# The scan step of a two-layer selective state-space network: from a ScalarE clamp with B corrections to one saturating add on VectorE

## What is computed

```python
xr, gate = jnp.split(x @ W_in.T, 2, axis=-1)
xc = silu(causal_conv4(xr + t_emb) + b_conv)
xn = layernorm(xc) * ln_g + ln_b                      # 512 channels
Bm, Cm, dt = jnp.split(xn @ W_xproj.T, 3, axis=-1)    # 16 states each
Ad = 1.0 + tanh(dt @ W_dt.T + b_dt) * 0.01 * -tanh(A_log)
Bd = Bm * jnp.minimum(norm(xn), 1.0)
def step(h, inputs):
    ad, bd, xt, ct = inputs
    h = jnp.clip(h * ad[:, :, None] + bd[:, :, None] * xt[:, None, :], -10.0, 10.0)
    return h, jnp.einsum('bd,bdh->bh', ct, h)         # h: 16 states x 512 channels
y = scan(step) + D * xn
x = x + y * silu(gate) @ W_out.T
```

## Time and profile before

| what | value |
|---|---|
| median of 3 runs | 1794.24 us |
| lowest and highest run | 1790.63 and 1795.34 us |
| span of the profiled execution, first to last instruction | 1790.3 us |
| median less the span | 3.9 us |
| TensorE busy | 1677.0 us, 94% |
| VectorE busy | 1623.9 us, 91% |
| ScalarE busy | 1307.1 us, 73% |
| GpSimd busy | 686.9 us, 38% |
| mean granted TensorE clock | 0.988 |

### The profile page before, as it was taken

How to read it: one execution, slowest core, us unless ns; L and a number is a source line. 1 busy time by engine, 2 the same in 40 slices (tenths; PEclk the granted TensorE clock), 3 DMA queues, 4 the chain that set the end, 5 groups by cost and what they waited for, 6 DMA issues and landing times. The chain is left out here.

```text
span 1790.3 us, 43798 instructions
## 1 busy us (share of the span) xinstructions
PE 1677.0 (94%) x14852; PEld 748.9 (42%) x14852; DVE 1623.9 (91%) x2492; ACT 1307.1 (73%) x2213; POOL 686.9 (38%) x702
## 2 busy tenths in 40 slices
PE   6999999999999999889999999999998899999998
PEld 3555555555554555332222224545553322222244
DVE  5899999999987999989999998679999899999975
ACT  5655556455546999889999993069998899999910
POOL 0223233232332332456666650012335576765500
PEclk9999999999999999899999999999998999999999
DMA  4000001000002344554545666624345445455678
GB/s 162 1 2 0 1 2 31 2 1 0 1 1 83 129 161 163 181 172 133 183 150 188 226 188 205 237 84 173 136 175 185 155 137 184 150 189 196 189 235 276
DMA packets 126456, 226.85 MB, mean 127 GB/s; under 512 B 35620, under 2 KB 61220, under 8 KB 117540
## 3 DMA queue, kind: packets, MB, share of 16 engines
q1 hardware_dynamic: 125912, 223.51, 37.9%
q10 hardware_dynamic: 432, 1.84, 0.3%
HBM read 141.95 MB, written 83.36 MB: 126 GB/s over the span
## 5 line engine op out<-in xcount | busy, mean ns | idle before, releaser
L1063 ACT ACTIVATE R<-q,Ast 128x512 f32<-128x512 f32 x1016 | 632.9, 708 | 34.5 <-DVE q L2085 32.3
L2085 DVE SCALAR_TENSOR_TENSOR q<-R,PS 128x512 f32<-128x512 f32 x1008 | 610.3, 677 | 9.6 <-ACT R L1063 5.9
L628 POOL TENSOR_TENSOR Uw<-Ub,rowmask 96x512 bf16<-96x512 bf16 x256 | 335.6, 1345 | 144.0 <-PE PS L1510 131.7
L1510 PE MATMUL PS<-xq,Uw 97*128 97x512 bf16 x1024 | 327.1, 391 | 46.5 <-DVE q L2085 37.8
L1527 PE MATMUL PS<-q,Wy 128*32 128x512 f32 x2016 | 279.8, 610 | 0.4 <-DVE q L2085 0.4
L1510 PEld LDWEIGHTS PS<-xq,Uw 97*128 97x128 bf16 x1024 | 84.9, 97 | 363.5 <-DVE q L2085 271.4
L1178 PE MATMUL PS<-X,Win 128*128 (+1 forms) x456 | 213.6, 606 | 0.1
L1079 PE MATMUL PS<-xn,Wl 128*128 128x512 f32 x384 | 186.6, 609 | 0.8 <-DVE xn L1649 0.7
L549 POOL TENSOR_TENSOR ex<-ex,rs 128x1024 f32<-128x1024 f32 x32 | 76.8, 2401 | 164.2 <-DVE rs L1672 164.2
L1767 DVE SCALAR_TENSOR_TENSOR acc<-xp,Wc,acc 128x512 f32<-128x512 f32 x192 | 134.5, 749 | 2.6 <-DVE eC L1889 0.2
L542 POOL TENSOR_TENSOR vsc<-vTd,vs_t 128x1024 f32<-128x1024 f32 x16 | 41.6, 2601 | 216.4 <-ACT vTd L773 216.4
(11 more groups left out here) (183 smaller groups left out, 2640.9 us busy)
## 6 DMA issues: line engine op xcount, KB each, us to landing
xq<-xpart_d SPq DMA_DIRECT2D x384, 192.0 KB
sg_d<-sg SPq DMA_DIRECT2D x16, 1024.0 KB, 5.3
xn_d<-z SPq DMA_DIRECT2D x16, 1024.0 KB, 3.9
y_d<-ys SPq DMA_DIRECT2D x64, 256.0 KB, 4.0
xnp<-xn_d SPq DMA_DIRECT2D x16, 1024.0 KB, 8.3
sgp<-sg_d SPq DMA_DIRECT2D x16, 1024.0 KB, 11.1
xpart_d<-xh SPq DMA_DIRECT2D x16, 512.0 KB, 2.9
xpart_d<-xmi SPq DMA_DIRECT2D x16, 512.0 KB, 3.7
```

What stands on the lines that cost most here:

```text
L628: pl.tensor_tensor(Uw[0:XROWS, h, w, :, :, :], Ub[0:XROWS, w, 0:N, ds(s0, CH)].rearrange("p n t -> p t n").unsqueeze(2).broadcast_to([XROW ...
L1063: act.activation((end if end and (h, t) == (1, CH - 1) else R)[:, w, :], q[:, t % 2, w, :], ACT.Relu, scale=Ast[:, h, w, t:t + 1], bias=CL ...
L1510: pe.matmul(PS[:, w, :], Uw[0:KROWS, h, w, t, :, :].rearrange("p b n -> p (b n)"), xq[0:KROWS, hb, w, s8 % XT, :], start=True, stop=True). ...
L2085: v.scalar_tensor_tensor(out=q[:, s8 % 2, w, :], in0=R[:, w, :], scalar=2 * CLIP, in1=PS[:, w, :], op0=ALU.min, op1=ALU.subtract).then_inc ...
```

## The change

The state is kept as it is. VectorE does the whole step in one instruction, a custom operation of two tensors and two constants: q = max(min(R + PSUM, 10), -10). ScalarE only scales: R = decay * q, and does so for token n out of the q of token n - 1, right before step n. With it go: the division of B by the decay (GpSimd's four instructions a group, a reciprocal and the factor mr on VectorE), `carried`, `fold_b` on TensorE, the strip `By` and its matmuls and staging, the 97th row, the clamps after the last token. `y_of` reads q of its own token. The x buffers are free as soon as the input matmul has read them, and SP's loads wait for that instead of for `y_of`. The custom instruction stands in no loop: VectorE's eights of tokens are all written out; ScalarE's, TensorE's and GpSimd's loops stay. The copy of y comes one token earlier (after tokens 1 and 5 of an eight instead of 2 and 6).

```diff
-                def over_decay(it):
-                    pl.wait_ge(am_r, it + 1)
...
                 def stage(...):
-                    pl.tensor_tensor(By[0:XROWS, h, :, :, MID:MID + GB],
-                                     Ub[0:XROWS, :, N:NB, ds(s0, CH)].rearrange("p g o t -> p t g o").broadcast_to([XROWS, CH, QW, GB]),
...
-                stage(1, 0, 0)
-                for p in range(2):
-                    pl.wait_ge(ac_r, l * (PASSES * QW * S) + QW * S - QW + 2 * p + 2 + READY)
-                    alone(pl)
-                    pl.tensor_scalar(R_end[:, 2 * p:2 * p + 2, :], R_end[:, 2 * p:2 * p + 2, :], 2 * CLIP, -CLIP, ALU.min, ALU.add).then_inc(ep_q, 1)
-                stage(1, 0, 1)
+                stage(1, 0, 0, True)
+                stage(1, 0, 1, True)
...
-                def clamp(pi, c2, first, between=None, end=None):
+                def decayed(pi, c2, first, between=None):
                     for h in range(2):
                         cn = pi * CHUNKS + c2 * 2 + h
                         act.wait_ge(pl_a, cn + 1)
...
                         for t in range(CH):
                             if between:
                                 between(c2 * 8 + h * CH + t)
+                            if first and h == 0 and t == 0:
+                                continue
                             for w in range(QW):
-                                act.wait_ge(dv_q, cn * (QW * CH) + QW * t + w + 1 + QW)
-                                act.activation((end if end and (h, t) == (1, CH - 1) else R)[:, w, :], q[:, t % 2, w, :], ACT.Relu,
-                                               scale=Ast[:, h, w, t:t + 1], bias=CLIP).then_inc(ac_r, 1)
+                                act.wait_ge(dv_q, cn * (QW * CH) + QW * t + w + 1)
+                                act.activation(R[:, w, :], q[:, (t + 1) % 2, w, :], ACT.Copy,
+                                               scale=Ast[:, h, w, t:t + 1]).then_inc(ac_r, 1)
...
-                def fold_b(it):
-                    pe.wait_ge(rB_r, it + 1)
-                    pe.matmul(PS[:, 7, 0:P], ident[:, :], rB[:, :], start=True, stop=False)
-                    pe.wait_ge(eC_r, it + 1)
-                    pe.matmul(PS[:, 7, 0:P], fold[:, :], eC[:, :], start=False, stop=True).then_inc(tok_mm, 1)
...
                     for p in range(2):
...
                         for w in (2 * p, 2 * p + 1):
-                            mm = pe.matmul(PS[32 * w:32 * w + 32, 4 + h, :], By[0:XROWS, h, t, w, MID - t * GB:MID + (CH - t) * GB],
-                                           xq[0:XROWS, hb, w, xt, :], start=False, stop=(t == CH - 1), skip_group_check=True)
+                            mm = pe.matmul(PS[32 * w:32 * w + 32, 4 + h, :], Wy[:, h, w, t * 32:(t + 1) * 32],
+                                           q[:, s8 % 2, w, :], start=(t == 0), stop=(t == CH - 1), skip_group_check=True)
...
-                    v.tensor_tensor(rB[:, :], PS[:, 6, 0:P], mr[:, :], ALU.mult).then_inc(rB_r, 1)
-                def carried(it):
+                    v.tensor_tensor(rB[:, :], PS[:, 6, 0:P], mn[:, :], ALU.mult).then_inc(rB_r, 1)
...
-                    v.tensor_copy(tvp[:, 0, :], PS[:, 7, 0:P]).then_inc(tv_s, 1)
+                    v.tensor_copy(tvp[:, 0, :], rB[:, :]).then_inc(tv_s, 1)
...
-                        v.scalar_tensor_tensor(out=q[:, s8 % 2, w, :], in0=R[:, w, :], scalar=2 * CLIP, in1=PS[:, w, :],
-                                               op0=ALU.min, op1=ALU.subtract).then_inc(dv_q, 1)
+                        v._custom_dve(bass.dve_ops.TENSOR_ADD_SAT, out=q[:, s8 % 2, w, :], in0=R[:, w, :], in1=PS[:, w, :],
+                                      s0=CLIP, s1=-CLIP).then_inc(dv_q, 1)
...
-                        if s8 == 2 and before:
+                        if s8 == 1 and before:
                             keep_y(pi, c2 * 2 - 1, 1)
-                        if s8 == 6:
+                        if s8 == 5:
                             keep_y(pi, c2 * 2, 0)
...
-                    with v.Fori(plain, CHUNKS // 2) as c2:
+                    for c2 in range(plain, CHUNKS // 2):
                         eight(pi, c2, False, True)
-                pi = l * PASSES + PASSES - 1
-                for p in range(2):
-                    v.wait_ge(ac_r, pi * (QW * S) + QW * S - QW + 2 * p + 2 + READY)
-                    v.tensor_scalar(R[:, 2 * p:2 * p + 2, :], R[:, 2 * p:2 * p + 2, :], 2 * CLIP, -CLIP, ALU.min, ALU.add).then_inc(ep_q, 1)
                 keep_y(l * PASSES + PASSES - 1, CHUNKS - 1, 1)
```

More of the change, by code:

```diff
@@ L155, in cond_resid_kernel @@
         zq = sb("zq", [P, DC, TOK], where=front)
-        rc0 = sb("rc0", [P, P], where=front)
+        sb("rc0", [P, P], where=front)
         zve = sb("zve", [P, P], where=front)
@@ L167, in cond_resid_kernel @@
         mn = sb("mn", [P, P], where=front)
-        mr = sb("mr", [P, P], where=front)
+        sb("mr", [P, P], where=front)
         dts = sb("dts", [P, P], where=front)
@@ L196, in cond_resid_kernel @@
         ys = sb("ys", [P, 2, DI], where=scan)
-        R_end = sb("R_end", [P, QW, DI], where=scan)
+        spare_y = sb("spare_y", [P, QW, DI], where=scan)
         scan.close()
@@ L658, in _ @@
                     alone(pl)
-                    stage(0, 0, h, True)
+                    stage(0, 0, h, True, True)
                 last_parts(l * G + G - 2)
@@ L1055, in clamp @@
                         act.wait_ge(pl_a, cn + 1)
-                        if first and h == 0 and between:
-                            act.wait_ge(pe_yq, pi * (2 * S) + USED)
                         for t in range(CH):
@@ L1069, in _ @@
                     for c2 in range(plain):
-                        clamp(pi, c2, c2 == 0, last_group if ps == 0 else None)
-                    with act.Fori(plain, CHUNKS // 2 - 1) as c2:
-                        clamp(pi, c2, False)
-                    clamp(pi, CHUNKS // 2 - 1, False, end=R_end if ps == 0 else None)
+                        decayed(pi, c2, c2 == 0, last_group if ps == 0 else None)
+                    with act.Fori(plain, CHUNKS // 2) as c2:
+                        decayed(pi, c2, False)
         @block.tensor
@@ L1539, in _ @@
                     for c2 in range(plain):
-                        for s8 in range(1, 9):
+                        for s8 in range(8):
                             if ps == 0:
@@ L1543, in _ @@
                             inputs(pi, c2, s8 + 1, ps == 0 and c2 == 0)
-                            if ps and s8 == 1:
-                                y_of(pi - 1, CHUNKS // 2 - 1, 8, last=R_end, spare=(0, 0))
                             y_of(pi, c2, s8)
                     with pe.Fori(plain, CHUNKS // 2 - 1) as c2:
-                        for s8 in range(1, 9):
+                        for s8 in range(8):
                             inputs(pi, c2, s8 + 1)
                             y_of(pi, c2, s8)
-                    for s8 in range(1, 8):
+                    for s8 in range(8):
                         if s8 < 7:
```

162 lines of the change are left out of this document (58 added, 104 removed).

## The result

| | before | after |
|---|---|---|
| median of 15 runs, us | 1792.12 (1788.21 to 1797.58) | 1798.59 (1794.32 to 1804.05) |
| span of the profiled execution, us | 1790.3 | 1802.3 (its time 1804.05) |
| granted clock of TensorE, mean | 0.988 | 0.981 |

The ratio after to before is 1.0032, with a 95% interval of 1.0021 to 1.0044: slower by 6.5 us, just past what can be told from no change. The forecast was 1779.3 us. So some 19 us are to be explained. None of them lies where I had put most of the risk, in the pace of the custom instruction. A costlier start of pass 0 with less gained behind it was among my rivals, at 0.05 and with 1787 us; the rest I hadn't seen.

What follows compares the result with a forecast made beforehand. The scan was taken to run at VectorE's pace, ScalarE second. Terms 0 - 3.9 + 4.2 - 7.7 - 4.0 - 3.5 = -14.9 us gave a span of 1775.4, median 1779.3 us; range 1769 to 1800.

Steps and rivals of the forecast that it cites:

- A costlier start of pass 0 with less gained behind it: Rival: start costs +8.4 instead of +4.2 us, nothing gained from the reorder at step 17; 1787 us, chance 0.05.
- Steady state: Scan: VectorE's instruction count per token unchanged, custom step at the old pitch of 0.598 us; 0 us.
- The two rivals to which I gave 0.30: Scan: custom instruction clearly slower (0.17; half-way 1809, at most 1839 us) or slightly slower (0.13; 11 ns each, 1790 us).
- Front: Seven bodies a layer: without mr and eC `rows` starts 0.28 us earlier in each; -3.9 us in all.
- The rest of the body hangs on `rows`: Front body: z waits for the spreading of `rows`, so its 0.28 us earlier start counts in full.
- Start of pass 0: ScalarE's `high` and `middle` stand ahead of the R for steps 1 and 2; +2.1 us a layer, +4.2 in all.
- Steps 14 to 17: Pass 0: reciprocal, eC and mr gone from VectorE, `split_b` needn't wait for TensorE's fold; -3.8 us a layer, -7.7 in all.
- ScalarE carries them on: Pass 0 up to step 13: ScalarE, the tighter engine, passes on the start's 2.1 us a layer.
- Between the passes: VectorE's idle time while TensorE's y waits for GpSimd's clamp of the last R goes; -2.0 us a layer, -4.0 in all.
- end: End of the scan: y is copied without waiting for R, the clamp and a second round; -1.75 us a layer, -3.5 in all.
- The written-out loop: VectorE's scan: written-out steps take 9.65 us for sixteen, looped 9.64, so neither branch nor fetch shows; costed at nothing.
- The clock rival: TensorE's clock falls in the scan; 35 tokens at the low level would bring +35 us, 1814, all +256; chance 0.05.

Runs made afterwards that it cites:

- second pair of profiles: Kernel before and changed kernel, each run again with no edit: 1792.1 us, ratio 1.0011, and 1796.4 us, ratio 1.0026.
- run 3: Changed kernel with GpSimd's xlo waiting for VectorE's mean rows instead of rB: 1790.9 us, ratio 0.9988 to the kernel before.
- run 4: Changed kernel with the last group's pieces on ScalarE one token later, behind the decays: 1789.6 us, ratio 0.9972 to the kernel before.
- both edits: Changed kernel with xlo waiting for the mean rows and ScalarE's pieces one token later: 1784.4 us, 0.9957; with VectorE's scan looped, 1780.8 and 1779.9 us.

## Why the prediction was wrong

The measured 1798.6 us lies within the stated range of 1769 to 1800, but by luck: its slow end was made for a slower custom instruction, and that isn't what happened. By the prediction's own steps, with the measured value of the second pair of profiles:

- **Steady state, 0: right.** The pitch is 0.598 us and the loop's turns don't show in the scan. The two rivals to which I gave 0.30, a slower custom instruction, fall with it. So does the sentence from the Trainium skill's "Vector Engine (DVE) Microarchitecture Reference", section 3.4, by which I had estimated 608 ns: sixteen take 9.64 us, and the measurement decides. The sentence there speaks of one kind of custom program, with integer inputs, so it was a distant source.
- **Front, -3.9: wrong, +5.0.** Two things failed. "The rest of the body hangs on `rows`" was wrong: before the change `rows` was done 0.3 us ahead of the projections behind which TensorE spreads it, and run 3 shows what the term is worth without anything else, 0.06 us a body. And I had not asked what GpSimd would do with an earlier release. Run 3, which takes it away, gains 2.5 us a front. Removing eC took away not just its 0.29 us but also the thing that kept xlo off `rows`.
- **The last body and `split_b`.** The source of the casts moved from PSUM to SBUF. I costed that at nothing. In the last body of the front it costs 0.7 us (3.20 instead of 2.54 from the first cast to step 0, beside GpSimd's `Uw`), and in the scan of layer 0 the first cast takes 0.73 instead of 0.29 us, again until GpSimd's `Uw` is through. This is read from the rows; it wasn't tried apart.
- **Start of pass 0, +2.1 a layer: right.** `rows` stands 10.8 us behind step 0 instead of 8.4. Run 4 takes away this very delay.
- **Steps 14 to 17, -3.8 a layer: right in size, wrong in what is left of it.** From am to the start of `split_b` it takes 9.4 us, and took 13.2: -3.8. But am itself stands 47.8 us behind step 0 instead of 44.0. Of these 3.8 us the start explains 2.4; "ScalarE carries them on" was too kind, as steps 4 to 13 add 1.4. And from the start of `split_b` to the last `xr`, VectorE takes 20.6 us instead of 18.5: the casts cost 0.5 more, and the waits for R before steps 17 and 20 are 0.80 and 0.50. "I count all of it" was the error: the same misplaced pieces on ScalarE hold up the later steps too, and run 4, which moves them all, gives 3.8 and 3.9 us in the two layers.
- **Between the passes -2.0 and end -1.75 a layer: right**, 3.9 together.
- **Behind the scan, 0: wrong, +4.0 and -0.6.** No term stood for it. What is shown: it isn't the DRAM place of `ones`, nor the removed loads, nor the custom instruction, nor the written-out loop alone. The full DMA engines move some 30 GB/s less for 30 us, and one instruction packet delays two landings. Why they move less stays open.
- **The written-out loop, 0: too good.** In three pairs with the new program the looped kernel is faster: 5.3 and 3.9 us on one chip each, and 0.9940 against 0.9957 on two; in the old program by 0.9 us, with an interval that takes in 0 and 4. The intervals of the last three pairs overlap, but the sign is the same four times. The scan's own stages don't show it, and I can't say which instructions wait.

In sum the front is 8.9 us off, pass 0 8.1 and the stages behind the scans 3.4, in part through the loop; pass 1 and the start take 0.1 off. From -14.9 that leads to the measured +5.3. The clock rival was not it where I had put it: in the steady scan the granted clock is 1.00. But in pass 0, where steps wait, TensorE is part of the time at the low level, and longer after the change: the mean granted clock there is 0.94 in both layers, against 0.95 and 0.96 before (second profiles), an estimate of 22 and 22 us at the low level against 18 and 14. In run 3, whose pass 0 is 1.1 us shorter with the same code, it is 0.96 and 0.95. So a part of the 1.4 us between steps 4 and 13 may be the clock's; no run separates it from ScalarE's order.

The best version here is the changed kernel with both edits and VectorE's loop kept: 1780 us, 0.9933 of the kernel before, though its interval overlaps those of the written-out versions. That is where the forecast had the change itself, though by other terms.

## What to carry to other kernels

When a change removes an instruction on which another engine waited, ask what that engine starts now, and beside which instruction: the removed wait may have been the spacing between them. Before you count an earlier result as a gain, look at what its consumer has queued ahead of it. And when the engine that feeds the scan gets its work in another order, place each small piece behind the work that the bottleneck waits for; here that was worth 6.7 us, nearly as much as the small instructions and the wait that the change took from steps 14 to 17 (3.8 us in each layer).

## What the runs showed of the hardware

- **Some VectorE instructions with all their tensors in SBUF wait beside a running GpSimd instruction.** Beside GpSimd's TENSOR_TENSOR, a 128x128 one took 1.29 instead of 0.34 us (`rows`) and 0.70 to 1.26 instead of 0.22 us (the cast of rB); VectorE's instructions with a PSUM input kept their time beside it (xr 0.68, z 2.48 for four, the cast out of PSUM 0.28). One xlo takes 4.56 / 4 = 1.14 us, and `rows` ended 1.30 us after the first began: that is the whole of it and then its own run, nearly. The Trainium skill, "SBUF — State Buffer", section "Who interferes with whom", has a rule for `rows`: a VectorE instruction with two SBUF inputs contends with a GpSimd one that reads SBUF, for ports that only one of them holds at a time. The trace agrees, with those numbers. For the cast, which has one SBUF input, the measured times stand by themselves. The rule would have warned of the change of xlo's wait.
- **A custom saturating add on VectorE runs at the pace of the built-in two-tensor form**: 677 ns each, 0.598 us apart.
- **An instruction packet among large loads** goes with two landings 0.8 and 1.6 us later (5.6 and 8.8 against 4.8 and 7.2 us), far more than its own 0.5% of the engines' time in that window of 4 us. With the packet moved away by 64 or 32 empty instructions elsewhere in the program, the delay of the two was gone.
- **Semaphore increments in a full VectorE queue cost nothing that shows**: one ahead of each add left pass 1 at 165.8 us.
- **Full DMA engines don't always move the same**: with the same loads in the same order, at a share of 1.03 or more of the 16 engines, 290 GB/s in one program and 330 in another. The runs don't show why.
